# A graph convolution computed as (A x) W1 instead of A (x W1), in a fused four-layer graph network

## What is computed

```
x = _layernorm(x + _L0_gnn_ref(x, adj, ...))     # relu([x, (adj x)/deg] W^T)
x = _layernorm(x + _L1_gnn_ref(x, adj, ...))     # attention-weighted transition, 3 hops
x = _layernorm(x + _L2_gnn_ref(x, adj, ...))     # the layer that the change touches
x = _layernorm(x + _L3_gnn_ref(x, adj, ...))     # 8-head attention, scores times 2*adj

def _gcn_layer(x, adj, W, b):
    support = jnp.einsum('bnf,fh->bnh', x, W)
    return jnp.einsum('bnm,bmh->bnh', adj, support) + b
# layer L2:
x = jax.nn.relu(_gcn_layer(batch_graph, adj, W1, b1))
x = jax.nn.relu(_gcn_layer(x, adj, W2, b2))
out = _gcn_layer(x, adj, W3, b3)
```

## Time and profile before

| | us |
|---|---|
| median of 3 runs | 3142.06 (3141.99 to 3142.89) |
| the profiled execution | 3141.49 |
| its span, first to last instruction | 3139.7 |
| PE busy | 3023.2 |
| DVE, ACT, POOL busy | 2090.6, 1724.4, 448.6 |
| mean granted TensorE clock | 0.992 |

### The profile page before, as it was taken

The page is one execution under the profiler, slowest core; times in us unless marked ns, Lnnn a source line. Parts: engine busy times, 40 slices in busy tenths (PEclk is TensorE's granted clock), DMA queues, the critical chain, the costliest instruction groups (busy, mean ns, idle before and its releaser), DMA issues.

```text
span 3139.7 us, 71133 instructions
## 1 busy us (share of the span) xinstructions
PE 3023.2 (96%) x28188; PEld 2645.5 (84%) x28188; DVE 2090.6 (67%) x4060; ACT 1724.4 (55%) x3048; POOL 448.6 (14%) x1666
## 2 busy tenths in 40 slices
PE   6999999999999999999999999999999999999999
PEld 5988789877898788987889877898778987789877
DVE  4637976379762797627976389753887538874388
ACT  3525855258542684526844278442784337853377
POOL 0101211012110121101211012111121111211112
PEclk9999999999999999999999999999999999999999
DMA  5022131121321213202133021330213302133010
GB/s 218 30 79 65 49 145 54 57 70 44 144 77 37 67 52 135 96 22 67 49 135 108 12 71 44 134 108 14 69 52 125 108 14 72 49 125 108 24 42 19
DMA packets 145270, 234.50 MB, mean 75 GB/s; under 512 B 12839, under 2 KB 113964, under 8 KB 144940
## 3 DMA queue, kind: packets, MB, share of 16 engines
q1 hardware_dynamic: 144940, 229.96, 22.3%
HBM read 120.86 MB, written 83.89 MB: 65 GB/s over the span
## 4 chain that ended last, share of the span: by engine, by line
PE 87%; DVE 7%; ACT 3%; issue 2%; SPq 1%; POOL 1%; DMA 0%; DVEq 0%; POOLq 0%; ACTq 0%
PE ps L506 16%; PE ps L508 16%; PE ps L507 16%; PE ps L734 15%; PE ps L724 9%; PE ps L752 8%; PE ps L605 1%; DVE t_lo L1228 1%; PE ps L765 1%; PE ps L564 1%; PE ps L595 1%; DVE al_area L1371 1%; DVE u_hi L1385 1%; ACT t_hi L931 1%; PE ps L705 0%
## 5 line engine op out<-in xcount | busy, mean ns | idle before, releaser
L1525 DVE CUSTOM_DVE_ANT_0 r<-ps,adjn 128x1024 f32<-128x1024 f32 x512 | 620.7, 1212 | 18.9 <-DVE xr L1572 10.3
L1172 ACT ACTIVATE r<-r,nmax 128x1024 f32<-128x1024 f32 x512 | 584.8, 1142 | 23.0 <-POOL nmax L498 22.3
L506 PE MATMUL ps<-u_hi,t_hi 128*128 128x256 f32 x2048 | 588.6, 287 | 0.6
L508 PE MATMUL ps<-u_hi,t_lo 128*128 128x256 f32 x2048 | 579.3, 283 | 0.0
L507 PE MATMUL ps<-u_lo,t_hi 128*128 128x256 f32 x2048 | 578.9, 283 | 0.0
L734 PEld LDWEIGHTS ps<-ident,r 128*128 128x128 f32 x4096 | 462.5, 141 | 115.4 <-issue 77.4
L734 PE MATMUL ps<-ident,r 128*128 128x128 f32 x4096 | 536.8, 274 | 7.2 <-DVE pt L1541 7.0
L1541 DVE COPY pt<-ps 128x512 f32<-128x512 f32 x512 | 352.9, 689 | 93.4 <-PE ps L734 73.8
L931 ACT ACTIVATE pt<-ps 128x512 f32<-128x512 f32 x512 | 304.0, 594 | 176.5 <-PE ps L734 158.2
L506 PEld LDWEIGHTS ps<-u_hi,t_hi 128*128 128x128 f32 x2048 | 391.5, 191 | 4.0 <-DVE t_lo L1228 4.0
L507 PEld LDWEIGHTS ps<-u_lo,t_hi 128*128 128x128 f32 x2048 | 391.4, 191 | 0.0
(11 more groups left out here) (165 smaller groups left out, 5237.2 us busy)
## 6 DMA issues: line engine op xcount, KB each, us to landing
adjn<-in_adj SPq DMA_DIRECT2D x64, 512.0 KB, 3.4
t_spill<-t_hi SPq DMA_DIRECT2D x64, 512.0 KB, 5.9
t_spill<-t_lo SPq DMA_DIRECT2D x64, 512.0 KB, 6.0
t_hi<-t_spill SPq DMA_DIRECT2D x32, 1024.0 KB, 5.4
t_lo<-t_spill SPq DMA_DIRECT2D x32, 1024.0 KB, 8.1
xn<-in_x SPq DMA_DIRECT2D x16, 512.0 KB, 4.2
x_spill<-xn SPq DMA_DIRECT2D x64, 128.0 KB, 1.7
q_stack<-u_hi SPq DMA_DIRECT2D x64, 128.0 KB, 2.5
```

The source lines that it names most:

```text
L506: pe.matmul(dst, a_hi, b_hi, start=first, stop=False, skip_group_check=check)
L508: return pe.matmul(dst, a_lo, b_hi, start=False, stop=last, skip_group_check=check)
L1172: act.activation(r[:, s % RSLOTS, :], r[:, s % RSLOTS, :], ACT.Exp, bias=nmax[:, s % 4:s % 4 + 1], accum_out=prow[:, qt % 2, h:h + 1]).the ...
L1525: dve.tensor_tensor_reduce(out=r[:, s % RSLOTS, :], in0=ps[:, 2 * (s % 2):2 * (s % 2) + 2, :].rearrange("p a c -> p (a c)"), in1=adjn[:, q ...
```

## The change

The first convolution of layer 2 is computed as (A x) W1. The normalised rows `xn` are split directly: ACT copies them to `row_hi`, DVE the remainder to `row_lo`, 256 columns a row tile (views of the `xt` memory, free after layer 1's last projection). They are the stationary operand of the 96 products with `t`, which need features as output partitions, and so need no transposition. The node tile 7 comes last for both feature tiles. The sum (features on partitions, nodes along columns) is split into `agg_hi`, `agg_lo` (views of the `u` memory) and then projected by 24 matmuls of 512 columns with W1 stationary ("mix", 4 units of 6) into the PR banks, from which `hidden` reads. The 16 transposes and the 48 matmuls of 256 columns are gone. In the diff, cut to its core:

```diff
+        row_hi = xt_hi[:, :, :].rearrange("p f n -> p (f n)").rearrange("p (t f) -> p t f", f=F)
+        agg_hi = u_hi[:, :].rearrange("p (f n) -> p f n", n=N)
...
             def pr_bank(b, n):
-                if n >= 2 and PR_ORDER[n - 2][0] == "z":
+                if n >= 2 and PR_ORDER[n - 2][0] == "mix":
+                    pe.wait_ge(h_raw, nth(b, 8, PR_ORDER[n - 2][1] + 1))
+                elif n >= 2 and PR_ORDER[n - 2][0] == "z":
...
# PE
-                    if t == NT - 3:
-                        pe.wait_ge(acc_free, nth(b, 3 * NT, NT + 2))
-                        transpose_x_half(b, 2, 0)
-                project_pairs(b, "conv 0", W_G1, xt_wait(b, 2), range(1))
-                transpose_x_late(b, 2, 1)
-                project_pairs(b, "conv 0", W_G1, xt_wait(b, 2), range(1, 2))
-                transpose_x_late(b, 2, 2)
-                project_pairs(b, "conv 0", W_G1, xt_wait(b, 2), range(2, PAIRS))
-                pe.wait_ge(acc_free, nth(b, 3 * NT, 2 * NT))
                 for half in range(HALVES):
+                    pe.wait_ge(acc_free, nth(b, 3 * NT, 2 * NT - 2 + 2 * half))
                     for k in range(BLOCKS // 2 * half, BLOCKS // 2 * (half + 1)):
                         pe.wait_ge(t_in[k], nth(b, 32, 32))
+                    for ft, j in ([(ft, j) for ft in range(FT) for j in range(NT - 1)] +
+                                  [(ft, NT - 1) for ft in range(FT)]):
+                        if half == 0 and (ft == 0 or j == NT - 1):
+                            pe.wait_ge(rows_ready, nth(b, NT, j + 1))
+                        at = slice(half * 512, (half + 1) * 512)
+                        last = three(ps[:, ACC + 2 * half + ft, :], row_hi[:, j, ft * P:(ft + 1) * P],
+                                     row_lo[:, j, ft * P:(ft + 1) * P], t_hi[:, j, at], t_lo[:, j, at], j == 0, j == NT - 1)
+                        if j == NT - 1:
+                            last.then_inc(acc_full, 1)
+                for k in range(2 * FT):
+                    half, ot = k // FT, k % FT
+                    pe.wait_ge(agg_ready, nth(b, 2 * FT, FT * (half + 1)))
+                    at, o = slice(half * 512, (half + 1) * 512), slice(ot * P, (ot + 1) * P)
+                    dst = pr_bank(b, pr["mix", k])
                     for ft in range(FT):
+                        last = three(dst, w_hi[:, W_G1, ft, o], w_lo[:, W_G1, ft, o], agg_hi[:, ft, at],
+                                     agg_lo[:, ft, at], ft == 0, ft == FT - 1)
+                    last.then_inc(pr_full, 1)
...
# ACT
                 for t in range(NT - 3):
                     normalise(b, 1, t)
-                x_transposed(b, 2, 0)
...
+                act.wait_ge(pr_full, nth(b, PR_UNITS, pr["h", NT - 1] + 1))
+                rounded_rows(range(NT - 3))
+                for t in range(NT - 3, NT):
+                    normalise(b, 1, t)
+                    rounded_rows(range(t, t + 1))
+                for k in range(2 * FT):
+                    half, ft = k // FT, k % FT
+                    act.wait_ge(acc_full, nth(b, AF_PER, AF_C1 + k + 1))
+                    copy(agg_hi[:, ft, half * 512:(half + 1) * 512], ps[:, ACC + k, :]).then_inc(agg_act, 1)
+                hidden(b, 0)
...
# DVE, in the loop over the row tiles t of layer 1
+                        if t == NT - 2:
+                            rows_rest(range(NT - 3))
                         dve.wait_ge(acc_full, nth(b, AF_PER, AF_P2 + t + 1))
...
-                    if t == NT - 3:
-                        x_transposed(b, 2, 0)
...
+                    if t == NT - 2:
+                        rows_rest(range(NT - 3, NT - 2))
+                rows_rest(range(NT - 2, NT))
+                for k in range(2 * FT):
+                    half, ft = k // FT, k % FT
+                    at = slice(half * 512, (half + 1) * 512)
+                    dve.wait_ge(agg_act, nth(b, 2 * FT, k + 1))
+                    rest(agg_lo[:, ft, at], ps[:, ACC + k, :], agg_hi[:, ft, at], agg_ready)
                 hidden(b, 0)
```

More of the change, by code:

```diff
@@ L56, in build_program @@
     TP_L1 = x_units(1, 0) + late_units(1) + [("al", part, t) for part, t in AL]
-    TP_ORDER = TP_L0 + TP_L1 + sum([x_units(layer, 0) + late_units(layer) for layer in (2, 3)], [])
+    TP_ORDER = TP_L0 + TP_L1 + x_units(3, 0) + late_units(3)
     tp = {unit: n for n, unit in enumerate(TP_ORDER)}
@@ L76, in build_program @@
                 [("z", k) for k in range(PAIRS)] + [("h", t) for t in range(NT)] +
-                [(f"conv {c}", k) for c in range(3) for k in range(PAIRS)] +
+                [("mix", k) for k in range(2 * FT)] + [(f"conv {c}", k) for c in (1, 2) for k in range(PAIRS)] +
                 [("qk", part) for part in QK[:4]] + [("values", 0)] + [("qk", part) for part in QK[4:]] +
@@ L193, in build_program @@
         ul = u_lo[:, :].rearrange("p (t f) -> p t f", f=F)
+        row_hi = xt_hi[:, :, :].rearrange("p f n -> p (f n)").rearrange("p (t f) -> p t f", f=F)
+        row_lo = xt_lo[:, :, :].rearrange("p f n -> p (f n)").rearrange("p (t f) -> p t f", f=F)
+        agg_hi = u_hi[:, :].rearrange("p (f n) -> p f n", n=N)
+        agg_lo = u_lo[:, :].rearrange("p (f n) -> p f n", n=N)
         f32 = lambda ap: ap.bitcast(F32)
@@ L244, in build_program @@
         xr_free = sem("xr_free")
+        rows_hi = sem("rows_hi")
+        rows_ready = sem("rows_ready")
+        agg_act = sem("agg_act")
+        agg_ready = sem("agg_ready")
         h_raw = sem("h_raw")
@@ L349, in build_program @@
         AF_L0, AF_P2, AF_C1, AF_C2, AF_C3, AF_PER = 0, NT, 2 * NT, 2 * NT + 4, 2 * NT + 8, 3 * NT + 8
-        U_G, U_Z, U_C, U_PER = 0, PAIRS, 2 * PAIRS, 5 * PAIRS
+        U_G, U_Z, U_C, U_PER = 0, PAIRS, 2 * PAIRS, 4 * PAIRS
         LN_PER = 4 * NT
@@ L860, in _ @@
-                pe.wait_ge(acc_free, nth(b, 3 * NT, 2 * NT))
                 for half in range(HALVES):
+                    pe.wait_ge(acc_free, nth(b, 3 * NT, 2 * NT - 2 + 2 * half))
                     for k in range(BLOCKS // 2 * half, BLOCKS // 2 * (half + 1)):
                         pe.wait_ge(t_in[k], nth(b, 32, 32))
-                    for ft in range(FT):
[L865 to L869, removed]
+                    for ft, j in ([(ft, j) for ft in range(FT) for j in range(NT - 1)] +
[7 more added lines that the diff above has]
+                            last.then_inc(acc_full, 1)
@@ L988, in rows_from_pr, with hidden @@
                     copy(u_hi[:, k * 512:(k + 1) * 512], ps[:, PR + n % 2, :]).then_inc(u_act, 1)
-            def hidden(b, c, af):
+            def hidden(b, c):
                 for k in range(2 * FT):
                     n, half, ft = 4 * c + k, k // FT, k % FT
-                    act.wait_ge(acc_full, nth(b, AF_PER, af(k)))
+                    if c == 0:
+                        act.wait_ge(pr_full, nth(b, PR_UNITS, pr["mix", k] + 1))
+                    else:
+                        act.wait_ge(acc_full, nth(b, AF_PER, AF_C2 + k + 1))
                     if n >= 2:
                         act.wait_ge(h_ready, nth(b, 8, n - 1))
-                    act.activation(ev[:, n % 2, 0:512], ps[:, ACC + k, :], ACT.Relu,
+                    src = ps[:, PR + pr["mix", k] % 2, :] if c == 0 else ps[:, ACC + k, :]
+                    act.activation(ev[:, n % 2, 0:512], src, ACT.Relu,
                                    bias=cols[:, c, ft:ft + 1]).then_inc(h_raw, 1)
@@ L1108, in _, with rounded_rows @@
                         copy(u_hi[:, (k - 1) * 512:k * 512], ev[:, (k - 1) % 2, 512:1024]).then_inc(u_act, 1)
+                def rounded_rows(ts):
+                    for t in ts:
+                        act.wait_ge(ln_done, nth(b, LN_PER, NT + t + 1))
+                        copy(row_hi[:, t, :], xn[:, t, :]).then_inc(rows_hi, 1)
                 for t in range(NT - 3):
                     normalise(b, 1, t)
-                x_transposed(b, 2, 0)
[L1113 to L1123, removed]
+                act.wait_ge(pr_full, nth(b, PR_UNITS, pr["h", NT - 1] + 1))
[8 more added lines that the diff above has]
+                hidden(b, 0)
                 rows_from_pr(b, "conv 1")
-                hidden(b, 1, lambda k: AF_C2 + k + 1)
+                hidden(b, 1)
                 rows_from_pr(b, "conv 2")
@@ L1315, in hidden @@
                     dve.wait_ge(h_hi, nth(b, 8, n + 1))
+                    if c == 0:
+                        dve.sem_inc(pr_free, 1)
                     rest(xt_lo[:, ft, at], ev[:, n % 2, 0:512], xt_hi[:, ft, at], h_ready)
@@ L1446, in _, with rows_rest @@
                         rest(u_lo[:, at], ev[:, (k - 1) % 2, 512:1024], u_hi[:, at], u_ready)
+                def rows_rest(ts):
+                    for t in ts:
+                        dve.wait_ge(rows_hi, nth(b, NT, t + 1))
+                        rest(row_lo[:, t, :], xn[:, t, :], row_hi[:, t, :], rows_ready)
                 for t in range(NT + 1):
@@ L1460, in _ @@
                         tile_stats(b, 1, t)
```

(8 more changed lines are left out.)

## The result

| | before | after |
|---|---|---|
| median, us | 3142.06 (5 runs, 3141.32 to 3143.99) | 3127.91 (5 runs, 3122.05 to 3128.81) |
| profiled execution, its span | 3141.49, 3139.7 | 3126.85, 3125.1 |
| PE busy | 3023.2 | 3012.0 |

The ratio is 0.9951, with a 95% interval from 0.9939 to 0.9963: 0.5% faster, 14 us. The forecast was 18 us faster, 3124.0: the measured 3127.91 lies outside the forecast's own range (3121 to 3126) and inside its 80% range (3120 to 3131).

What follows compares the result with a forecast made beforehand. PE's own stream was taken as the bound. 7.91 us removed less 5.62 added, less 0.03 for a restart, gives 2.26 us an element, 18.1 over eight: 3124.0 us, own range 3121 to 3126, 80% range 3120 to 3131.

Steps and rivals of the forecast that it cites:

- The terms of PE's stream: Layer 2's first convolution: 7.91 us removed, 5.62 us of matmuls added, products unchanged at 21.79; 2.29 us saved an element.
- the rival built on its columns alone: Layer 2's transposes: each worth only 0.059 us, so 1.4 us saved an element, 3130.8 us; chance 0.04.
- The waits: Waits added in layer 2's first convolution: all hidden, row tile 6 with 1.4 us to spare, tile 7 under 9.5 us.
- The relus: After the products: ACT's relu and copy take 1.35 us a unit against PE's 1.40, so ACT keeps up.
- these 0.3 us stay: Conv 1's third pair: its wait of 0.3 us was to remain, the same four steps standing in the same order.
- The reload: The adjacency's last block before half 1: cover shrinks from 10 to 3.4 us, still hidden at the longest landing, 9.3 us.
- Rival 4: Adjacency reload: last block lands too late for half 1; at 15 us PE waits 4.7 us, 3161 us; chance 0.03.
- Rival 1: Relu chain, projection to conv 1: tighter than worked out, PE waits some 0.6 us an element, 3128.8 us; chance 0.15.
- what goes here goes 8 times: From the stage to the kernel: 2.26 us saved in each of 8 elements makes 18.1 us in all.

Runs made afterwards that it cites:

- few_transposes: The kernel before with 10 of the 16 transposes of layer 2's input left out, so it works on stale values: 3135.29 us, one time.
- relu_slow: The changed kernel with one more ACT copy of 512 columns in each of the four relu units of the first convolution: 3138.41 us, one time.
- late_reload: The changed kernel with the last reloaded adjacency block issued only when half 0's sums are complete: 3212.08 us, one time.
- after_warm: The changed kernel with 22 matmuls that feed nothing ahead of the first transposes of x in elements 1 to 7: 3120.47 us, ratio 0.9930 to before.
- after_again: The changed kernel run and profiled again without any edit: 3126.70 us, ratio 0.9950 to before.

## Why the prediction was right, and by how much it was off

**The terms of PE's stream** held. 24 matmuls in 5.60 us (0.233 each; 5.62 worked out), 96 products in 21.78, 7.91 us removed: the stretch is 33.14 us, where the forecast's terms give 35.45 - 7.91 + 5.62 = 33.16. The 0.03 us set aside for a restart after a wait was not spent, since no wait is left. From the first product to conv 1's first matmul are 27.38 us (27.4 forecast). A transpose is worth 0.109 us (few_transposes), and the rival built on its columns alone falls. The formula of the Trainium skill, TensorE: Matmul & The Clock Gate, section Back-to-back issue gap, says 56 ns for an isolated matmul of 128 columns, and the same section about 81 ns for one in a stream of loads and matmuls; the trace agrees with neither, with 109.

**The waits** all lay hidden. The order of DVE's queue came out as worked out:

```profile
551.10 1.78 DVE L1252 TENSOR_TENSOR xt_lo<-xn,xt_hi 128x256 fp32r<-128x256 f32 x5
552.80 0.47 DVE L1489 SCALAR_TENSOR_TENSOR ev<-ps,rdeg,ev 128x256 f32<-128x256 f32 x1
...
557.15 0.39 DVE L1252 TENSOR_TENSOR xt_lo<-xn,xt_hi 128x256 fp32r<-128x256 f32 x1
559.69 0.43 DVE L1252 TENSOR_TENSOR xt_lo<-xn,xt_hi 128x256 fp32r<-128x256 f32 x1 [2.15 <-ACT xt_hi L945]
```

Taken from the start of the products, 555.23: the first five remainders are through 2.35 us ahead (2 worked out, with 0.415 us a remainder where 1.78 / 5 = 0.36 was measured); row tile 6 is through 2.3 us after it and row tile 7 4.9 us after it, where PE wants them 4.1 and 9.5 us after it. The wait that stood there before is gone.

**The relus** keep pace with the projection as forecast. ACT's timeline:

```profile
578.61 0.69 ACT L1015 ACTIVATE ev<-ps,cols 128x512 f32<-128x512 f32 x1 [0.80 <-PE ps L516]
579.34 0.63 ACT L945 ACTIVATE xt_hi<-ev 128x512 fp32r<-128x512 f32 x1
580.01 0.69 ACT L1015 ACTIVATE ev<-ps,cols 128x512 f32<-128x512 f32 x1
```

A unit takes 1.40 us (1.35 worked out), PE's own pace, with no idle time between two of them. Unit 0's relu ends at 579.30, 2.3 us after the projection's start, as worked out, and PE needs its bank 2.8 us after it. Only the wait of conv 1's third pair grew, by 0.06 us, where "these 0.3 us stay" was said. relu_slow shows how near this is.

**The reload.** The last block's second DMA was issued at 555.82, and the DMA share fell to 0.09 in the window from 563:

```profile
555.82 0.58 SPq L402 DMA_DIRECT2D t_lo<-t_spill  x1
...
562.00:563.00 1.00, 1.00 (x6) 0.80 (x6) 0.00 (x0) 0.00 (x0) 0.00 (x0) 1.00 0.84 265
563.00:564.00 1.00, 1.00 (x6) 0.84 (x5) 0.00 (x0) 0.00 (x0) 0.00 (x0) 1.00 0.09 31
```

It had landed by about 563, against the 566.1 at which half 1 begins. Rival 4 was priced by late_reload and is not in play.

**Rival 1's time** (3128.8) is nearer to the measured 3127.91 than the forecast's, but that is chance: PE has no idle entry in the projection or at conv 1's start, which is where that rival would show.

**What was mis-sized** is the step from one element to the kernel: "each later instruction of PE follows from it, so what goes here goes 8 times". 2.26 times 8 gave 18.1. The trace has 17.3 (8 x 2.31 = 18.5, less 0.7 for the gaps of 0.33 us in two elements, less 0.06 x 8 for the third pair's wait). The rest, from 17.3 to the 14.2 and 15.0 us of the two comparisons of medians, is not in the touched stage. Three parts of the kernel move from run to run whatever the kernel: over the nine profiles, the start by 62.6 to 64.3 us, the attention part by 1084.1 to 1088.5, the changes of element by 248.5 to 253.6 where the clock may fall. Keeping the clock up moved the distance of the medians only from 15.0 to 15.5 us. The prediction took the one profiled execution of before as typical, and its start is the shortest of those compared. Whether the 2 us that are left are the spread of such runs (the changed kernel's ten times lie between 3121.8 and 3128.8) or a small loss that the change brings with it stays open; beyond the gaps and the third pair's wait, which are in the 17.3, the profiles show none that is the same in each.

The gap of 0.33 us in layer 1 of elements 4 and 6 does come with the change: it stands at the same two instructions in all six profiles of the changed kernel and its variants, and in none of the three with the old order. On PE it has no idle entry, but DVE's timeline shows where it starts. Here is the same instruction of after in element 1 and in element 4:

```profile
495.38 0.69 DVE L1397 CUSTOM_DVE_ANT_0 al_area<-al_area,adjn 128x512 f32<-128x512 f32 x1 [0.73 <-ACT al_area L1072]
...
1650.60 0.69 DVE L1397 CUSTOM_DVE_ANT_0 al_area<-al_area,adjn 128x512 f32<-128x512 f32 x1 [1.09 <-ACT al_area L1072]
```

DVE starts 0.36 us later, and PE's next transposes of `al_area` wait for it; in element 6 it is the reading of a row sum (L1464). Such pauses of DVE of about 0.35 us are in every profile. Counted through the trace, they stand at the 1727th, 3391st and 5055th of DVE's instructions in after, at the 2623rd, 3263rd, 3519th, 4927th and 5055th in before, the same places in every profile with the same DVE program (six and three), and always a multiple of 128 apart (waits counted too, the first is number 0). The change makes DVE's program 56 instructions longer, so that other work falls on these places; in before none of it held PE up. What DVE does in the pause no run shows.

The version with both edits, after_warm, is the fastest measured: 3120.47 us, 0.7% under the kernel before.

## What to carry to other kernels

Where one engine's stream is unbroken, count what a change takes from it and adds to it by distances from start to start, and then work out for each new wait how early its condition is met; this gave the stage to 0.05 us (2.26 worked out, 2.31 measured). Removing work that covers a wait gives back only part of its price (0.64 of 1.09 us here), unless the new order puts other work over that wait. And with a stage's gain known from two traces to 0.01 us, the kernel's time can still differ by several us through parts outside it: compare part by part before looking for a cause.

## What the runs showed of the hardware

- An idle time of 3.2 us on PE was followed by a stretch at the 1.2 GHz level at 6 of the 7 changes of element in before, at all 7 in after and at 5 in after_again. Filling it with 22 matmuls that feed nothing kept the clock at 1.00 at all seven and made both kernels 6 us faster.
- After a wait of 8.4 us inside a stage (late_reload), the lower level held on into the work: 48 matmuls of 512 columns took 13.3 us for 10.9.
- A transpose of 128 columns costs PE's stream 0.109 us, nearly as much as a matmul of 256 columns (0.118); a matmul of 512 columns costs 0.227 to 0.234.
- The lower level for 3.4 or 6.8 us at a change of element cost 0.4 to 1 us or 1.2 to 1.6 us, over 63 changes in nine profiles.
- DVE starts single instructions about 0.35 us late at fixed places of its program, multiples of 128 instructions apart, the same in each run. A change that moves other work onto such a place can lose that time far from the stage it touches: 0.33 us in each of two elements here.
